# Unread products on TensorE at stage borders, one later load, and a rounding by a product with one, in a fused kernel of five stages

## The reference, cut to what matters

```python
# x: (32, 64, 256), everything float32
c = cond(x)                    # 8 gated experts and a shared one: silu(x Wg) * (x Wu) @ Wd, F = 1024
x = x + hyp_attention(c)       # hyperbolic attention, 16 heads, causal, spike mask
# second branch
s0, s1 = relu(x @ swi[i]) @ swo[i]              # the two shared experts ("dense")
eo     = relu(x @ wi[type]) @ wo[type]          # "typed": the expert is given for each sequence
w      = softmax(relu([eo[:,0], s0[:,0], s1[:,0]] @ g1) @ g2)
h      = eo * w0 + s0 * w1 + s1 * w2            # "join"
y = h + rope_attention(conv3(layernorm(h)))     # rotary attention, 16 heads, causal ("rope")
n = layernorm(y)
e = argmax(n @ router_w)                        # one of 4 experts for each token
y = y + (silu(n @ Wv[e][:, :F]) * (n @ Wv[e][:, F:])) @ proj[e]     # "moe"
x = x + y
```

## Time and profile before

| | us |
|---|---|
| median of 3 runs | 2192.46 (2191.40 to 2193.07) |
| the profiled execution: own time | 2192.84 |
| the profiled execution: span | 2191.0 |
| mean granted TensorE clock over the span | 0.96 of full |
| busy: TensorE 2006.2, VectorE 1124.4, ScalarE 910.9, GpSimd 697.6 | 92%, 51%, 42%, 32% |

### The profile page before, as it was taken

The page is one execution under the profiler, slowest core; times in us unless marked ns, Lnnn a source line. Parts: engine busy times, 40 slices in busy tenths (PEclk is TensorE's granted clock), DMA queues, the critical chain, the costliest instruction groups (busy, mean ns, idle before and its releaser), DMA issues. The chain is left out here.

```text
span 2191.0 us, 34148 instructions
## 1 busy us (share of the span) xinstructions
PE 2006.2 (92%) x12638; PEld 1697.1 (77%) x12638; DVE 1124.4 (51%) x1964; ACT 910.9 (42%) x1898; POOL 697.6 (32%) x778
## 2 busy tenths in 40 slices
PE   7999999999999999999998767899999766959998
PEld 6888888888888888888887645788799544849997
DVE  3334434434434434433434687442488565847886
ACT  4242332424233242332423579322355354636564
POOL 3030210303012030200300068211298233968885
PEclk9999999999999999999999879899999877979999
DMA  5010010100001010020000300320066113556651
GB/s 166 1 45 14 1 57 0 58 0 30 27 0 57 0 57 0 0 84 0 0 1 0 78 2 3 116 77 10 29 210 215 47 38 117 179 197 199 201 190 55
DMA packets 95631, 140.30 MB, mean 64 GB/s; under 512 B 15310, under 2 KB 72560, under 8 KB 95536
## 3 DMA queue, kind: packets, MB, share of 16 engines
q1 hardware_dynamic: 88480, 123.02, 17.6%
q0 software_dynamic: 4928, 12.86, 1.7%
q10 hardware_dynamic: 2128, 3.15, 0.4%
HBM read 109.37 MB, written 12.06 MB: 55 GB/s over the span
## 5 line engine op out<-in xcount | busy, mean ns | idle before, releaser
L603 DVE TENSOR_TENSOR cond_h<-cond_silu,ps 128x512 f32<-128x512 f32 x288 | 198.1, 688 | 697.5 <-ACT cond_silu L514 694.1
L514 ACT ACTIVATE cond_silu<-ps 128x512 f32<-128x512 f32 x288 | 172.3, 598 | 771.8 <-PE ps L433 771.8
L433 PE MATMUL ps<-a_x_hi,cond_w_hi 128*128 128x512 f32 x1152 | 449.8, 390 | 2.0 <-DVE a_x_lo L265 2.0
L433 PE MATMUL ps<-a_x_lo,cond_w_hi 128*128 128x512 f32 x1152 | 449.2, 390 | 0.0
L433 PE MATMUL ps<-a_x_hi,cond_w_lo 128*128 128x512 f32 x1152 | 449.1, 390 | 0.0
L402 POOL TENSOR_TENSOR cond_w_lo<-cond_stage_up,cond_w_hi 128x256 fp32r<-128x256 f32 x144 | 108.7, 773 | 832.8 <-ACT cond_w_hi L495 832.8
L433 PEld LDWEIGHTS ps<-a_x_hi,cond_w_hi 128*128 128x128 f32 x1152 | 216.9, 188 | 47.4 <-DVE a_x_lo L265 2.4
L433 PEld LDWEIGHTS ps<-a_x_hi,cond_w_lo 128*128 128x128 f32 x1152 | 216.9, 188 | 45.2
L433 PEld LDWEIGHTS ps<-a_x_lo,cond_w_hi 128*128 128x128 f32 x1152 | 217.0, 188 | 45.0
L449 PE MATMUL ps<-cond_h_hi,cond_d_hi 128*128 128x512 f32 x576 | 224.4, 390 | 3.4 <-DVE cond_h_lo L571 3.4
L449 PE MATMUL ps<-cond_h_hi,cond_d_lo 128*128 128x512 f32 x576 | 224.1, 389 | 0.0
(11 more groups left out here) (378 smaller groups left out, 4019.9 us busy)
## 6 DMA issues: line engine op xcount, KB each, us to landing
moe_stage_up<-in_L_ffn_expert_wv SPq DMA_DIRECT2D x22, 1024.0 KB, 9.2
typed_stage_up<-in_L_cond_wi SPq DMA_DIRECT2D x11, 1024.0 KB, 5.0
typed_stage_dn<-in_L_cond_wo SPq DMA_DIRECT2D x11, 1024.0 KB
moe_stage_dn<-in_L_ffn_expert_proj SPq DMA_DIRECT2D x11, 1024.0 KB, 5.4
cond_stage_up<-in_L_cond_Wg SPq DMA_DIRECT2D x7, 1024.0 KB, 5.0
cond_stage_up<-in_L_cond_Wu SPq DMA_DIRECT2D x7, 1024.0 KB, 7.1
cond_stage_dn<-in_L_cond_Wd SPq DMA_DIRECT2D x7, 1024.0 KB, 5.5
rope_v_now<-rope_v_blk SPq DMA_DIRECT2D x16, 272.0 KB, 2.4
```

The costliest lines, as they stand in the source:

```text
L433: ins = pe.matmul(up_ps[st % 2][j], w[:, j, k, fs], x[:, k, tok], start=(i == 0), stop=(i == 3 * KC - 1))
L514: act.activation(silu[:, st % 2], up_ps[st % 2][0], ACT.Silu).then_inc(act_done, 1)
L603: dve.tensor_tensor(h[:, st % 2], silu[:, st % 2], up_ps[st % 2][1], ALU.mult).then_inc(up_free, 1)
```

## The change

It makes seven edits, A to G, and adds one helper.

- `keep_busy(pe, m, bank, times)` issues `times` products of the 128x128 identity with 512 columns of constants, in float32. Nothing reads what they write.
- A: at the end of `split_and_turn`, 3 of them, after ACT's copy out of bank 0 (a new semaphore `taken`).
- B: at the end of the typed stage, 5 (`LoadLate.tensor_late`).
- C: at the end of join, 8, after a wait for the last centring; and 2 ahead of the rope projections, between the waits for the weights and that for the source.
- D: behind the rope projections, 12.
- E: in the moe stage between the sort's last product and the first transposes of a gathered slot, 6.
- F: SP waits for the last gather of the typed stage before it loads the weights of join and rope.
- G: `d_hi` for odd f, in the typed and the moe stage, by a TENSOR_TENSOR with a column of ones in place of a copy. It is executed 44 times in each of the two stages.

```diff
@@ AttentionIn, tensor
                     pe.wait_ge(w.ready, 1)
+                    if not hyper:
+                        keep_busy(pe, m, m.bank[5], 2)
                     for i in range(NP):
...
                         ins.then_inc(spiked, 1)
+                    if not hyper:
+                        keep_busy(pe, m, m.bank[5], 12)
@@ join, tensor
                 steps((0, lambda t: turn(t + 2) if t + 2 < TT else None), (0, means), (1, variances))
+                pe.wait_ge(centred, TT)
+                keep_busy(pe, m, mean_ps[0], 8)
@@
+def keep_busy(pe, m, bank, times):
+
+    for _ in range(times):
+        pe.matmul(bank, m.ident, m.const[:, 0:TW], start=True, stop=True)
@@ class LoadLate
-    def __init__(self, *weights):
-        self.weights = weights
+    def __init__(self, m, slots, *weights):
+        self.m, self.slots, self.weights = m, slots, weights
+
+    def tensor_late(self, pe):
+        keep_busy(pe, self.m, self.m.bank[0], 5)
 
     def sync_late(self, sp):
+        sp.wait_ge(self.slots.x_loaded[(SLOTS - 1) % 2], 16 * (SLOT // P) * ((SLOTS + 1) // 2))
         for w in self.weights:
             w.load(sp)
@@ class SortFirst
         self.lists.find(pe)
+        keep_busy(pe, self.lists.m, self.lists.m.bank[3], 6)
@@ routed_ffn, end of tensor
                         down_half(f, (n - 1) % 2, i)
+                prelude.tensor_late(pe)
@@ routed_ffn, vector, round_dn
-                        dve.tensor_copy(d_hi[:, f], stage_dn[:, q, f]).then_inc(dn_rounded[1], 1)
+                        one = m.const[:, C_ONE:C_ONE + 1].to_broadcast([P, D])
+                        dve.tensor_tensor(d_hi[:, f], stage_dn[:, q, f], one, ALU.mult).then_inc(dn_rounded[1], 1)
@@ split_and_turn
                 ins.then_inc(turned, 1)
+            pe.wait_ge(taken, 1)
+            keep_busy(pe, m, m.bank[0], 3)
```

More of the change, by code:

```diff
@@ L2175, in tensor @@
     def tensor(self, pe):
+        pass
+    def tensor_late(self, pe):
         pass
@@ L2600, in _ @@
                 ins.then_inc(turned, 1)
+            pe.wait_ge(taken, 1)
+            keep_busy(pe, m, m.bank[0], 3)
         def take(eng, i, copy):
             eng.wait_ge(turned, i + 1)
-            copy(rows[:, 2 * i:2 * i + 2], m.bank[i].rearrange("p (j d) -> p j d", j=2))
+            ins = copy(rows[:, 2 * i:2 * i + 2], m.bank[i].rearrange("p (j d) -> p j d", j=2))
+            if i == 0:
+                ins.then_inc(taken, 1)
         @block.scalar
@@ L2731, in program @@
                                       a["L0_ffn_conv_w"])
-                routed_ffn(nc, m, "typed", False, slots, LoadLate(joining, rope))
+                routed_ffn(nc, m, "typed", False, slots, LoadLate(m, slots, joining, rope))
             join(nc, m, m.typed_rows, sent, m.sumT, s0, s1, joining, rope)
```

## The result

| | before | after |
|---|---|---|
| median, us | 2192.12 (2191.10 to 2194.59, 9 runs) | 2197.45 (2196.46 to 2201.31, 9 runs) |
| the profiled execution: own time, span | 2192.84, 2191.0 | 2196.46, 2194.7 |
| mean granted clock over the span | 0.960 | 0.970 |

The change makes the kernel slower: the ratio is 1.0025, with an interval of 1.0016 to 1.0035, 5.3 us by the medians. Forecast was 17.5 us faster. The clock is higher than before, and TensorE's busy share too (93% after 92%), and it did not help. One of the twelve runs of a later kernel, e1_copy_back, took 4087 us, for a reason that the record doesn't show, and is left out of that kernel's ratio.

What follows compares the result with a forecast made beforehand. TensorE, busy 92% of the span, was taken as the bound, leaving its waits and half-clock stretches to win. Terms -8.7 + 0.5 - 4.5 - 3.0 + 0.3 - 2.2 + 0.5 - 0.5 = -17.6 gave 2175 us; 8-in-10 range 2167 to 2186.

Steps and rivals of the forecast that it cites:

- G, moe: Moe stage: the product waits for one GpSimd operation at a time, not four; -8.7 us, bounds -11.4 and 0.
- Rival (a): Moe stage: the product waits for POOL as long as the copy did; the 8.7 us fall away, 2184; chance 0.18.
- G, typed: Typed stage: VectorE's extra 0.76 us a slot fits its room, POOL gives way more; +0.5 us, bounds 0 and +7.
- F: Last typed slot: gather lands within 6.6 us of issue, TensorE's 2.96 us wait goes; -4.5 us, bounds -5 and -1.5.
- the bound of -1.5: Last typed slot: the later load's smallest gain, if the slot's own weights are in the gather's way.
- C: Join to projections: hidden unread products win half of 5.9 us at half clock; -3.0 us, bounds -3 and +4.
- D: Behind the rope projections: barrier 0.3 us later, the clock falls once more; +0.3 us, bounds -2 and +8.
- B: End of typed, beside the scatter of the last slot's results; -0.5 us, bounds -1.6 and +0.5.
- E: Ahead of moe: about half of 4.97 us of half-clock work goes; -2.2 us, bounds -3 and +2.
- A: Ahead of dense: barrier 1.0 to 1.2 us later, some half-clock time comes back; +0.5 us, bounds -2.6 and +3.
- The forecast's mechanism for the clock: Borders between stages: unread products keep TensorE busy, bringing back the full clock; mostly half the slow stretch counted as gain.

Runs made afterwards that it cites:

- e1_copy_back: The changed kernel with the copy back in both routed stages; 2189.98 us (2189.78 without the run of 4087), ratio 0.9995.
- e2: The kernel before with only the product with one for odd d_hi, in the typed and moe stages; 2199.72 us, ratio 1.0043.
- e3: e1_copy_back without the 3 unread products ahead of dense; 2187.52 us, ratio 0.9988.
- e9: e8 with the gathers spread in the moe stage alone, both at step 1 in the typed stage; 2177.04 us, ratio 0.9941.
- e12: e9 with the product with one in place of the copy in the moe stage alone; 2176.40 us, ratio 0.9935.
- e8: e6 without the unread products at the end of typed, behind the rope projections and ahead of moe; 2174.41 us, ratio 0.9914.
- e11: e8 without SyncE's wait for the last typed gather before the later loads; 2175.90 us, ratio 0.9930.
- e4: e1_copy_back with each slot's second gather issued at step 4 instead of 1, in typed and moe; 2176.16 us, ratio 0.9929.
- e10: e8 without the unread products at the end of join and ahead of the rope projections; 2177.55 us, ratio 0.9938.
- e6: e4 without the 3 unread products ahead of dense; 2175.22 us, ratio 0.9916.

## Why the prediction was wrong, point by point

**G, moe: the step that failed.** The prediction read from 88 `moe_d_lo` with a longest of 1.54 us that a TENSOR_TENSOR waits for one operation of GpSimd, and a copy for all that are ready. That was a difference of place, not of form: `d_hi` is the first of its group and meets the run's start, `d_lo` comes behind it, when the run is over. The product waited 4.68 us at the copy's place, where the copy had 4.86. -8.7 was forecast, +4.6 came (e2: +4.3): 13 of the 22 us by which the forecast was off. Not all of the +4.6 is the product's: a first slot of 21 us, 1.9 of it, came in both traces with the product, but also in one of the three with the copy (e3), so that 2.4 to 2.7 (e2, changed kernel) is what can be put down to the form. A row that spoke against it was in sight: the 2.21 us of a `typed_d_lo`, more than any one operation of GpSimd there. Rival (a) named the right mechanism and gave it a price of nothing; but with the long run in it a steady slot hangs on VectorE, and the slower form came out at 0.2 us a slot.

The lock of which the Trainium skill speaks (SBUF — State Buffer, "SBUF: two separate sides") treats both forms alike, and in that the traces agree: 4.89 and 5.94 us at worst. They don't agree that the holder is whoever comes first, for one instruction: the operation of VectorE came 0.7 us into GpSimd's first one and waited for four. In the typed stage the two engines mostly took turns.

**G, typed.** +0.5 was forecast with bounds 0 and +7. With F in both, 144.24 against 142.76 and 142.31: +1.5 to +1.9; without F, +3.6. Slot by slot, leaving out the first and the last two, which F also touches, the changed kernel is 3.2 us longer than before and e2 2.9; 1.8 of either is the one slot of 13.8 us, and the copy has one of 13.6 in e3. The rest, 1.1 to 1.4, is twice the forecast or more.

**F.** -4.5 was forecast; in the sum of the typed stage -0.5 to -1.0 came (e9 and e12 against before, e8 against e11). The step to the last slot shows the term by itself: 16.64 us before and 14.07 in the changed kernel (e3: 13.97), where the clock stayed full behind the wait, but 15.68 to 16.08 in e1, e9 and e12, where it fell. So F gave 0.6 to 2.7 us. The gather was not there within 6.6 us of its issue: issued at 1685.02, it let TensorE start at 1693.41. The reason that was given for the bound of -1.5 fits, though no run tests it: the last slot's own weights, two loads of 1 MB, are issued at 1682.81 and 1684.82, and SP issues nothing else before 1693. TensorE's wait goes from 2.96 to between 1.8 and 2.4 us.

```profile
1693.41 0.66 PE L2387 MATMUL ps<-const,typed_x_row 128*128 128x128 f32 x4 [1.90 <-DMA typed_x_row<-typed_table,slot_source]
```

**C** was right in kind and nearly in size: -3.0 forecast, -2.5 in the trace; over the other traces it is 0.7 to 2.5. Its ten products are hidden, as worked out; TensorE is at the projections' first product 0.25 us after the source:

```profile
1770.20 7.57 PE L2174 MATMUL ps<-const 128*128 128x512 f32 x16
1779.35 1.95 PE L2174 MATMUL ps<-const 128*128 128x512 f32 x4 [1.58 <-PEq L89]
1781.55 0.51 PE L1081 MATMUL ps<-rope_wq_hi,rope_src_hi 128*128 128x512 f32 x1 [0.25 <-DVE rope_src_lo L1173]
```

**D** was right: +0.3 forecast, 0.1 in the gap before the units. **B**: -0.5 forecast, 0. **E**: -2.2 forecast, -0.3. The clock was there, but the first slot is set by others, it seems by VectorE and GpSimd, which have nine `w_lo` to work off: TensorE waited 3.91 us for `moe_h_lo` later in it. GpSimd there, in the timeline of after:

```profile
1966.94 11.20 POOL L2347 TENSOR_TENSOR moe_w_lo<-moe_stage_up,moe_w_hi 128x512 fp32r<-128x512 f32 x9
1980.97 5.01 POOL L2347 TENSOR_TENSOR moe_w_lo<-moe_stage_up,moe_w_hi 128x512 fp32r<-128x512 f32 x4
```

**A**: +0.5 forecast, +2.0 came. 1.0 is the later start of dense, which was in the forecast and came in one of the four traces with A; the dense stage's own 1.0 (up to 1.6 over the traces) was not thought of: a faster start in front of a wait makes the wait longer (2.03 us and not 0.60), and behind it the clock falls.

So the step that failed is the wait assumed for G in the moe stage, one operation of GpSimd where four were waited for. The forecast's mechanism for the clock was right and mostly mis-sized, by taking half of a slow stretch as gain although other engines set the pace there; the largest term rested on a wrong reading of why one instruction waits.

What stays open: why in two traces (e4, e10) the units take 101 to 102 us instead of 99.3; what decides in which execution a typed slot of 13.6 to 13.8 or a first moe slot of 21.1 to 21.2 us comes, since both are seen with either form; and how GpSimd and VectorE settle who is next, that is why VectorE was let in between ready operations in the typed stage and never in the moe stage. A GpSimd run broken by waits, with the gathers left in place, was not tried.

## What to carry to other kernels

Before giving a waiting instruction another form, find an instruction of the new form at the same place against the same neighbour; a group of the new form at another place proves nothing. Where the timeline shows VectorE's operations on SBUF waiting through a run of GpSimd's, shorten the run (spread what builds its backlog) before touching VectorE. And half-clock stretches behind a border are worth half their length only if TensorE, not the engine that feeds it, ends them.

## What the runs showed of the hardware that was not expected

An operation of VectorE whose operands all lie in SBUF, of whichever of the two forms tried, could wait through six back-to-back operations of GpSimd (4.3 us) in the typed stage, and through four (4.6 to 4.9 us) in each steady slot of the moe stage, though mostly it was let in after one in the typed stage. It counts as busy all the while: 4.0 of 17.06 us a moe slot. Operations with an input in PSUM took their 0.42 us beside the same run. The lowest ratio, e8's, is 0.9914 of the kernel before, 19 us faster (e6 is level with it), and moving one transfer's issue on GpSimd alone gives 0.9935, 14 us.
